# Flash-style cross attention on one core: value sums of eight heads in one PSUM bank, exponentials of 1536 columns, 4 of 40 units as a polynomial on VectorE, the four leftover keys in one tile

## The chip, the cores and the metric

The kernel runs on one core of a Trainium2 chip. The metric is the device time of one execution in microseconds (us). The engines are TensorE (PE, matrix products; its weight loads are listed apart as PEld), ScalarE (ACT, here the exponentials), VectorE (DVE), GpSimd (POOL, here copies of values) and SyncE (SP, which issues most DMAs). SBUF is the on-chip memory, PSUM the eight banks of 128 x 512 floats into which TensorE writes.

## What is computed

The reference is a decoder of four layers on 1024 query rows of width 128 and a context of 6404 rows. Three of the four layers (L0, L1, L3) have softmax attention with 16 heads of 8 channels over the whole context; L1 also attends causally to the queries themselves. Between the attention stages stand feed-forward layers that the change doesn't touch.

```python
# 16 heads of 8 channels, x: 1024 rows, ctx: 6404 rows, a mask over the keys
q = x_norm @ Wq + bq ; k = ctx @ Wk + bk ; v = ctx @ Wv + bv
scores = einsum("qhd,khd->hqk", q, k) * 8 ** -0.5      # L1: 1024 more keys, causal
out = softmax(scores, axis=-1) @ v                     # per head
x = x + tanh(gate) * (out @ Wo + bo)
```

## The kernel before

**Tiling.** The context is cut into 51 chunks of 128 keys (`NC`); the last holds only 4 keys (`LAST`). An attention stage is four sweeps (`SWEEPS`): eight of the sixteen heads (`hh`) by 512 of the 1024 queries (`qh`). A sweep goes over all 51 chunks; in L1 four or eight chunks of own keys (`nx`) follow, the later of them over fewer and fewer columns, with one more product with a triangular tile (`stair`) that masks them. Twelve sweeps make 612 chunks of context and 24 of own keys. A *unit* is one head by one chunk, 128 keys x 512 queries. A chunk has eight units.

**Scores.** A unit's score is one matmul (L1517) over 35 rows: even heads use the upper half of the array's rows (from 0), odd heads the lower half (from 64). Two units, an even and an odd one, make a pair; a pair fills two PSUM banks, and three such slots (banks 0 to 5) are used in turn. `scores(b, c, j)` waits for the exponential of three pairs ago.

**Exponentials.** ACT makes one exponential for each pair (L1334), 1024 columns, four for each chunk. No maximum is taken off the scores (a branch that would do it is not entered with these inputs), and the sum of the exponentials comes from a column of ones among the values.

**Values.** Four units make a value batch (L1530): four matmuls in float32 with 32 columns of weights each, one on each quarter of the array's columns, over the 512 queries. A float32 matmul stands as two records in the trace, so a batch is eight. Batches of heads 0 to 3 add up in bank 6, those of heads 4 to 7 in bank 7. At a sweep's end DVE copies both banks out (L1736). Before the next sweep's first value batch PE waits for that copy.

**Order.** PE's order is written out: two pairs of scores, one value batch, two pairs, one batch, in a loop of three chunks (`TC`). Keys for the next chunks are loaded by SP (L1059, L1062: three DMAs for each chunk) into three buffers `kr`; POOL copies values into `vr` (L1207). In front of a stage SP loads the first three chunks of keys, then sends `bound` through a DMA (L1079) to DVE, which makes a flag (L1698) that PE, ACT and SP read before they begin the sweeps. DVE has no work within a sweep. ACT issues the constant rows of `kr` and the weights (L1270 to L1287) in the preparation ahead of the first stage. After a stage PE transposes `accs`, four blocks for each 128 queries (L1567).

## Time and profile before

| | before |
|---|---|
| median of three runs | 3404.56 us (3403.14 to 3406.20) |
| the profiled execution | 3407.25 us |
| its span, first to last instruction | 3405.3 us |
| mean granted TensorE clock | 0.948 of full speed |
| busy: PE, ACT, DVE, POOL | 3077.4, 2607.3, 355.2, 202.7 us |
| first exponential of stage L0 to the last copy of its sums | 189.50 to 953.99 us |

A busy share of PE counts matmuls with modelled ends, so it does not say that the array streams all that time. The three attention stages make up about 2400 us of the span, and within them the pattern of a chunk repeats over and over; what a change of that pattern costs is read from one period of it.

### The profile page before, as it was taken

How to read it: one execution, taken by the hardware profiler on the slowest of the kernel's cores; microseconds unless marked ns; L12 is line 12 of the kernel's file. 1: busy time of each engine (PE TensorE's matmuls, PEld its weight loads, DVE VectorE, ACT ScalarE, POOL GpSimd, SP SyncE). 2: the span in 40 equal slices, each digit the busy share in tenths (PEclk: the TensorE clock that was granted, in tenths of full speed). 3: DMA queues.
4: the chain of work that ended last, by engine and by line, in shares of the span. 5: the costliest groups of instructions: out<-in, count | busy, mean ns of one | idle time of the engine just before them, and what ended most of it. 6: DMA issues, size and time to landing. Idle time of an engine off the chain costs nothing.

```text
span 3405.3 us, 62250 instructions
## 1 busy us (share of the span) xinstructions
PE 3077.4 (90%) x18851; PEld 1118.2 (33%) x18851; DVE 355.2 (10%) x951; ACT 2607.3 (77%) x3015; POOL 202.7 (6%) x726
## 2 busy tenths in 40 slices
PE   6689999999989799999999998969989999999988
PEld 3322222222233522222223224645622222222256
DVE  4410000000022500000000001342210000000021
ACT  3379999999933399699797994322289999999932
POOL 2000000000000000000000000010000000000000
PEclk9889999999979899799898997979999999999989
DMA  6701111111130011011010112101001111111100
GB/s 188 203 30 37 37 37 34 37 37 36 37 90 0 15 37 37 27 37 37 29 37 29 37 37 65 33 29 35 26 28 37 37 37 36 37 36 36 37 29 28
DMA packets 146162, 147.00 MB, mean 43 GB/s; under 512 B 15420, under 2 KB 98864, under 8 KB 146088
## 3 DMA queue, kind: packets, MB, share of 16 engines
q1 hardware_dynamic: 140304, 144.16, 13.8%
q10 hardware_dynamic: 5784, 1.88, 0.2%
q8 instruction: 43, 0.70, 0.1%
q14 instruction: 31, 0.25, 0.0%
HBM read 116.61 MB, written 29.37 MB: 43 GB/s over the span
## 4 chain that ended last, share of the span: by engine, by line
ACT 33%; issue 31%; PE 28%; ACTq 3%; DVE 3%; POOL 1%; DMA 0%; SPq 0%; DVEq 0%; POOLq 0%
ACT probs L1334 32%; PE PS L597 5%; PE PS L581 5%; PE PS L1530 3%; PE PS L1517 3%; PE PS L583 2%; PE PS L815 1%; ACTq L1329 1%; PE PS L803 1%; PE PS L1380 1%; ACTq L1338 1%; PE PS L1519 1%; PE PS L1390 1%; ACTq L1332 1%; PE PS L1444 1%
## 5 line engine op out<-in xcount | busy, mean ns | idle before, releaser
L1334 ACT ACTIVATE probs<-PS 128x1024 f32<-128x1024 f32 (+2 forms) x2544 | 2323.5, 1064 | 127.9 <-PE PS L1517 70.2
L1530 PE MATMUL PS<-probs,vr 128*32 128x512 f32 (+2 forms) x10176 | 1372.7, 612 | 135.5 <-ACT probs L1334 10.9
L1517 PE MATMUL PS<-qs,kr 35*128 35x512 f32 (+2 forms) x5088 | 985.2, 452 | 33.8 <-issue 15.7
L1517 PEld LDWEIGHTS PS<-qs,kr 35*128 35x128 f32 x5088 | 406.1, 189 | 1123.3 <-ACT probs L1334 1025.6
L1530 PEld LDWEIGHTS PS<-probs,vr 128*32 128x32 f32 x10176 | 203.0, 109 | 683.4 <-ACT probs L1334 645.6
L1207 POOL COPY vr<-vs 128x72 f32 (+1 forms) x636 | 159.7, 252 | 2881.8 <-PE PS L1530 2523.6
L1736 DVE COPY accs<-PS 128x1024 f32<-128x1024 f32 x12 | 14.7, 1225 | 2439.3 <-PE PS L1530 2439.3
L624 ACT ACTIVATE probs<-PS 128x512 f32<-128x512 f32 x96 | 57.3, 597 | 132.3 <-PE PS L581 71.8
L624 ACT ACTIVATE accs<-PS 128x512 f32<-128x512 f32 x96 | 57.3, 597 | 120.6 <-PE PS L581 63.2
L581 PE MATMUL PS<-xT,wide 128*128 128x512 f32 x256 | 125.6, 609 | 0.7 <-ACT xT L314 0.7
L597 PE MATMUL PS<-wide,accs 128*128 128x128 f32 x768 | 91.7, 281 | 5.0 <-DVE kf L656 5.0
L597 PEld LDWEIGHTS PS<-wide,accs 128*128 128x128 f32 x768 | 91.2, 198 | 11.5 <-issue 11.5
L597 PEld LDWEIGHTS PS<-wide,probs 128*128 128x128 f32 x768 | 88.3, 192 | 7.7 <-issue 7.7
L597 PE MATMUL PS<-wide,probs 128*128 128x128 f32 x768 | 88.3, 275 | 0.0
L768 ACT ACTIVATE probs<-PS,cols_w 128x512 f32<-128x512 f32 x48 | 32.8, 687 | 71.1 <-PE PS L804 71.1
L311 ACT ACTIVATE ln_sd<-ln_ve 128x8 f32<-128x8 f32 x8 | 1.7, 208 | 88.7 <-DVE ln_ve L285 88.7
L583 PE MATMUL PS<-xT,wide 128*128 128x512 f32 x128 | 66.7, 603 | 0.0
L581 PEld LDWEIGHTS PS<-xT,wide 128*128 128x128 f32 x256 | 46.7, 194 | 60.3 <-issue 33.8
L320 PE MATMUL PS<-ident,xn 128*128 128x128 f32 x64 | 17.0, 434 | 53.7 <-DVE xn L295 53.7
L656 DVE SCALAR_TENSOR_TENSOR kf<-PS,egate,kf 128x128 f32<-128x128 f32 x176 | 47.6, 344 | 153.8 <-PE PS L597 153.8
L581 PE MATMUL PS<-h_T,wide 128*128 128x512 f32 x128 | 59.9, 613 | 1.9 <-ACT h_T L933 1.9
L1244 ACT ACTIVATE kparts<-PS,bqk 128x384 fp32r<-128x384 f32 x27 | 16.0, 592 | 53.1 <-PE PS L1371 26.7
(269 smaller groups left out, 1206.5 us busy)
## 6 DMA issues: line engine op xcount, KB each, us to landing
kr<-key_pieces SPq DMA_DIRECT2D x1272, 64.0 KB
key_pieces<-kparts SPq DMA_DIRECT2D x36, 288.0 KB, 4.4
kr<-mask_strips SPq DMA_DIRECT2D x636, 4.0 KB
key_pieces<-probs SPq DMA_DIRECT2D x32, 288.0 KB, 4.7
vs<-values SPq DMA_DIRECT2D x2, 3672.0 KB, 15.5
values<-v_next SPq DMA_DIRECT2D x9, 432.0 KB, 5.3
wide<-in_L_ffn_w SPq DMA_DIRECT2D x28, 128.0 KB, 2.1
values<-probs SPq DMA_DIRECT2D x8, 432.0 KB, 5.3
```

What stands on the lines that cost most here:

```text
L581: last = te.matmul(PS[:, slot(m, k, i), :], eA[i][:, P * c:P * c + P], hT[:, 512 * half:512 * half + 512], start=True, stop=True)
L583: last = te.matmul(PS[:, 3 + slot(m, k, i), :], eB[i][:, P * c:P * c + P], hT[:, 512 * half:512 * half + 512], start=True, stop=True)
L597: last = te.matmul(PS[:, 6 + n // 4, n % 4 * P:n % 4 * P + P], moe_hid[i][:, S * c + P * n:S * c + P * n + P], eC[i][:, P * c:P * c + P], ...
L624: nc.scalar.activation(moe_hid[i][:, S * c + 512 * half:S * c + 512 * half + 512], PS[:, slot(m, k, i), :], m.func).then_inc(h_act, 1)
L656: last = v.scalar_tensor_tensor(moe_acc[:, P * n:P * n + P], o, g, moe_acc[:, P * n:P * n + P], ALU.mult, ALU.add)
L803: te.matmul(PS[:, u % 2, :], fw1[net][:, P * c:P * c + P], xT[:, cols], start=True, stop=True)
L815: last = te.matmul(o, fw2[net][:, D * c:D * c + D], hid[u % 4], start=(c == 0), stop=False)
L1207: g.tensor_copy(vr[b][:, :, 0:VC], vs[:, bass.ds(c, 1), h0:h0 + H // 2, :].rearrange("p o h v -> p (o h) v")).then_inc(v_copied, 1)
L1329: act.wait_ge(s_ready, 4 * c + (s.pairs + p + 1))
L1334: sc.activation(prob[p][:, :, q0:], PS[:, 2 * slot:2 * slot + 2, q0:], ACT.Exp, scale=SCALE).then_inc(p_ready, 1)
L1517: last = te.matmul(o, kr[b][own, j, :], qs[own, T8 // 2 * s.hh + j, 512 * s.qh + q0:512 * s.qh + 512], start=True, stop=not late)
L1530: last = te.matmul(PS[32 * j:32 * j + 32, 6 + g, q0:], vr[b][:, 4 * g + j, :], prob[2 * g + j // 2][:, j % 2, q0:], start=(first and c == ...
```

## The change

It rewrites the sweeps. Names: a *round* (`ITER`, 10 for each sweep) is five chunks, 40 units.

- The 4 keys of the last chunk leave the chunk pattern. All eight heads' leftover keys stand in one tile, `k_left`: four accumulating score matmuls (`left_scores`), one exponential of 512 columns (`exps_left`), one matmul of 128 columns of weights (`left_values`) for each sweep.
- ACT takes 36 units of a round in 12 groups of three (`GROUP`), each one exponential of 1536 columns; two slots of three banks (0 to 2, 3 to 5) are used in turn, so `scores(i, gr)` waits for the exponential of two groups ago. Four value buffers `prob` (`RING`) replace four of two units.
- The other four units (heads 0 to 3 of the third chunk) go to DVE: `score_d` writes one unit to bank 6, DVE reads it (L2077, L2079), and for two units at a time does five operations of 1024 columns (shift, three steps of a polynomial, the last product into `prob_d`, which lies in `accs`). `values_d` sums them with scaled values `vd`.
- All value batches add up in bank 7: the weights of a head are shifted by 16 of its 32 columns for heads 4 to 7.
- Base two: the query weights are scaled by `QSCALE`, ACT's scale is ln 2.
- Keys have five buffers; the third chunk's are loaded in three pieces. The leftover keys and values are loaded by 12 and 16 small DMAs in front of each stage, ahead of the DMA of `bound`. `wo` is turned through DRAM, with DMAs on ACT's queue.

```diff
+KB = 5
+ITER = (NC - 1) // KB
+GROUP = 3
+BY_ACT = ((0, 0), (0, 1), (1, 0), (1, 1), (2, 1), (3, 0), (3, 1), (4, 0), (4, 1))
+RING = 4
...
+                sp.wait_ge(v_final, a + 1)
+                load_left_values()
                 sp.wait_ge(bound_ready, a + 1)
                 sp.dma_start(bound_row[0:1, :], bound[32 * a:32 * a + H, 0:1]).then_inc(bound_in, 16)
...
-                            sc.activation(prob[p][:, :, q0:], PS[:, 2 * slot:2 * slot + 2, q0:], ACT.Exp, scale=SCALE).then_inc(p_ready, 1)
+                        sc.activation(prob[gr % RING], PS[:, bank:bank + GROUP, :], ACT.Exp, scale=LN2).then_inc(p_ready, 1)
...
+                    def scores(i, gr, first=False):
+
+                        if not (first and s.w == 0 and gr < 2):
+                            pe.wait_ge(p_ready, i * GPI + (s.groups + gr - 1))
...
+                    def score_d(i, j):
...
+                        if n or not isinstance(i, int):
+                            pe.wait_ge(d_read, i * DPI + n)
+                        score(PS[:, 6, :], 2, j).then_inc(d_ready, 1)
...
-                    with pe.Fori(1, NTILE) as i:
...
+                    with pe.Fori(1, ITER) as i:
+                        scores(i, 0)
+                        score_d(i, 0)
+                        values(s, i - 1, 7)
+                        scores(i, 1)
+                        values(s, i - 1, 8)
+                        scores(i, 2)
+                        scores(i, 3)
+                        score_d(i, 1)
+                        values(s, i, 0)
...
+                        scores(i, 5)
+                        score_d(i, 2)
+                        values(s, i, 2)
+                        scores(i, 6)
+                        values_d(s, i - 1)
...
+                        scores(i, 10)
+                        score_d(i, 3)
+                        scores(i, 11)
+                        values(s, i, 6)
...
+                    def two_units(i, p, first=False):
...
+                        if not (first and s.w == 0 and p == 0):
+                            dve.wait_ge(d_done, m - 1)
+                        for k in range(2):
+                            cols = slice(512 * k, 512 * k + 512)
+                            dve.wait_ge(d_ready, i * DPI + (n + k + 1))
+                            v.tensor_scalar(d_bits[:, cols], PS[:, 6, :], LOWEST, ROUND_AT, ALU.max, ALU.add).then_inc(d_round, 1)
+                            dve.wait_ge(d_round, i * DPI + (n + k + 1))
+                            v.scalar_tensor_tensor(d_x[:, cols], d_bits[:, cols], ROUND_AT, PS[:, 6, :], ALU.subtract, ALU.subtract).then_inc(d_read, 1)
+                        v.tensor_scalar(d_r.bitcast(I32), d_bits.bitcast(I32), 23, None, ALU.logical_shift_left).then_inc(d_shift, 1)
+                        dve.wait_ge(d_read, i * DPI + (n + 2))
+                        v.scalar_tensor_tensor(d_q, d_x, QA, d_x, ALU.add, ALU.mult).then_inc(d_q1, 1)
+                        dve.wait_ge(d_shift, m)
+                        v.scalar_tensor_tensor(d_bits, d_x, QC, d_x, ALU.add, ALU.mult).then_inc(d_q2, 1)
+                        dve.wait_ge(d_q1, m)
+                        v.scalar_tensor_tensor(d_q, d_q, QB, d_r, ALU.add, ALU.mult).then_inc(d_r1, 1)
+                        dve.wait_ge(d_q2, m)
+                        dve.wait_ge(d_r1, m)
+                        if s.w or not first:
+                            dve.wait_ge(d_used, i + ITER * s.w)
+                        v.scalar_tensor_tensor(prob_d[:, 2 * p:2 * p + 2, :].rearrange("p j n -> p (j n)"), d_bits, QD, d_q, ALU.add, ALU.mult).then_inc(d_done, 1)
```

PE, the loop of a sweep, before: half a chunk is two pairs (L1517) and a value batch (L1530).

```order
L1511 ISA
L1517 MATMUL PS<-qs,kr0 128x512 x2
L1511 REGISTER_ALU
L1517 MATMUL PS<-qs,kr0 128x512 x2
L1526 ISA
L1530 MATMUL PS<-probs,vr2 32x512 x4
```

PE, the same place in the changed kernel, from group 3 (`x3`, keys of chunk 1) over the second unit for DVE (the single matmul on `kr2`) to the batch after group 5. L1774 is a score, L1737 a value batch.

```order
L1774 MATMUL PS<-qs,kr1 128x512 x3
L1795 REGISTER_ALU
L1774 MATMUL PS<-qs,kr2 128x512
L1730 ISA
L1737 MATMUL PS<-probs,vr0 32x512 x4
L1780 REGISTER_ALU
L1774 MATMUL PS<-qs,kr1 128x512 x3
L1737 MATMUL PS<-probs,vr0 32x512 x4
```

A batch now follows one group of three units, not two pairs, and the single score stands in PE's queue ahead of batch 0, with its wait for DVE's second read of the unit before it (`d_read`).

DVE, the sweeps of the first stage, before, between the branch on the flag and the division that follows the stage: the four copies of the sums (L1736).

```order
L1729 CAST mparts<-mneg 128x128
L1731 TENSOR_TENSOR mparts<-mneg,mparts 128x128
L1701 UNCONDITIONAL_BRANCH
L1736 COPY accs<-PS 128x2x512 x4
L1740 RECIPROCAL rden<-PS 128x16
L1741 TENSOR_TENSOR xn<-PS,rden 128x128
```

DVE, one pair of units in the changed loop, with the semaphores that each row waits for. `kf`, `h_T`, `xT`, `xn` serve as scratch; `accs` is `prob_d`.

```order
L2077 TENSOR_SCALAR kf<-PS 128x512 [waits d_ready]
L2079 SCALAR_TENSOR_TENSOR h_T<-kf,PS 128x512 [waits d_round]
L2080 TENSOR_SCALAR xn<-kf 128x1024
L2082 SCALAR_TENSOR_TENSOR xT<-h_T 128x1024 [waits d_read]
L2084 SCALAR_TENSOR_TENSOR kf<-h_T 128x1024 [waits d_shift]
L2086 SCALAR_TENSOR_TENSOR xT<-xT,xn 128x1024 [waits d_q1]
L2091 SCALAR_TENSOR_TENSOR accs<-kf,xT 128x1024 [waits d_used,d_r1,d_q2]
```

What moved: between the reads of one pair of units and the reads of the next, DVE has five long operations in its queue, and PE's next `score_d` but one waits behind them. (The first two rows stand twice in the program, once for each unit.)

SP, in front of a stage, before: nine DMAs of keys, then `bound`.

```order
L1059 DMA kr2<-key_pieces 32x1x512 x2
L1062 DMA kr2<-mask_strips 2x512
L1079 DMA bound_row<-bound 1x16x1
L1081 TENSOR_LOAD flag
L1081 ISA x2
L1082 COMPARE_AND_BRANCH
```

SP, the same place in the changed kernel, from the last of four such groups of leftover keys on.

```order
L1158 DMA k_left<-key_pieces 16x4x4 x2
L1160 DMA k_left<-mask_strips 1x4x4
L1168 DMA v_left<-vs 4x9 x16
L1197 DMA bound_row<-bound 1x16x1
L1199 TENSOR_LOAD flag
L1199 ISA x2
L1200 COMPARE_AND_BRANCH
```

The DMA of `bound` now stands behind 40 more: 12 for keys, 12 for the leftover keys, 16 for the leftover values.

## Rows read from the trace of the kernel before

**Rows 1.** The page, busy time by engine (share of the span), instructions.

```profile
PE 3077.4 (90%) x18851; PEld 1118.2 (33%) x18851; DVE 355.2 (10%) x951; ACT 2607.3 (77%) x3015; POOL 202.7 (6%) x726
```

**Rows 2.** Timeline of ACT, first sweep: start, length, what, idle before.

```profile
205.60 175.19 ACT L1334 ACTIVATE probs<-PS 128x1024 f32<-128x1024 f32 x191 [0.33 <-PE PS L1517]
```

**Rows 3.** Timeline of PE, 700 to 702 us, full clock.

```profile
699.96 1.06 PE L1530 MATMUL PS<-probs,vr 128*32 128x512 f32 x8
700.96 0.73 PE L1517 MATMUL PS<-qs,kr 35*128 35x512 f32 x4
```

**Rows 4.** Timeline of PE, own keys of L1, full clock.

```profile
1616.66 0.50 PE L1517 MATMUL PS<-qs,kr 35*128 35x512 f32 x1
1617.09 0.23 PE L1519 MATMUL PS<-stair,ident_b 128*128 128x128 bf16 x1
```

**Rows 5.** Timeline of PE and of ACT, 577 to 583 us, half clock.

```profile
577.07 1.93 PE L1530 MATMUL PS<-probs,vr 128*32 128x512 f32 x8
578.93 1.22 PE L1517 MATMUL PS<-qs,kr 35*128 35x512 f32 x4
580.08 1.93 PE L1530 MATMUL PS<-probs,vr 128*32 128x512 f32 x8
...
582.78 1.94 ACT L1334 ACTIVATE probs<-PS 128x1024 f32<-128x1024 f32 x2 [1.07 <-PE PS L1517]
```

**Rows 6.** Groups by line and shape: count, busy us, mean ns (exponentials, operations of DVE).

```profile
L1334 ACT ACTIVATE probs<-PS 128x768 f32<-128x768 f32 x16 | 13.0, 811 | 11.1 <-PE PS L1519 11.1
L1334 ACT ACTIVATE probs<-PS 128x256 f32<-128x256 f32 x16 | 6.2, 384 | 21.0 <-PE PS L1519 21.0
L642 DVE TENSOR_TENSOR probs<-probs,PS 128x512 f32<-128x512 f32 x32 | 22.0, 688 | 61.5 <-ACT probs L624 61.5
L654 DVE TENSOR_SCALAR kf<-PS,egate 128x128 f32<-128x128 f32 x16 | 4.3, 343 | 29.9 <-PE PS L597 29.9
L1645 DVE TENSOR_SCALAR vs<-vs,valid_last 128x144 f32<-128x144 f32 x2 | 0.6, 284 | 0.0
```

**Rows 7.** Timeline of DVE between stages: dependent long operations, and eight independent short ones.

```profile
2119.48 1.23 DVE L873 TENSOR_TENSOR accs<-xn 128x1024 f32<-128x1024 f32 x1
2120.74 1.22 DVE L874 TENSOR_REDUCE ln_ve<-accs 128x8 f32<-128x1024 f32 x1
2151.84 2.16 DVE L656 SCALAR_TENSOR_TENSOR kf<-PS,egate,kf 128x128 f32<-128x128 f32 x8 [4.99 <-PE PS L597]
```

**Rows 8.** Timeline of PE over the end of the second sweep.

```profile
570.49 1.06 PE L1530 MATMUL PS<-probs,vr 128*32 128x512 f32 x8 [0.77 <-ACT probs L1334]
```

**Rows 9.** Windows: us, busy of PE, PEld, DVE, ACT, POOL, granted clock, DMA share, GB/s.

```profile
573.00:587.00 14.00, 13.74 (x58) 3.31 (x58) 0.00 (x0) 9.80 (x12) 0.50 (x2) 0.51 0.07 20
760.00:772.00 12.00, 9.66 (x72) 2.57 (x68) 1.23 (x1) 10.41 (x12) 0.76 (x3) 1.00 0.09 29
2867.00:2870.30 3.30, 3.30 (x16) 0.70 (x12) 0.00 (x0) 2.83 (x3) 0.00 (x0) 0.52 0.13 41
```

**Rows 10.** Timeline: first exponential and last copy of sums, stages L0 and L3.

```profile
189.50 1.02 ACT L1334 ACTIVATE probs<-PS 128x1024 f32<-128x1024 f32 x1 [10.52 <-PE PS L1517]
953.99 1.23 DVE L1736 COPY accs<-PS 128x1024 f32<-128x1024 f32 x1 [187.50 <-PE PS L1530]
2484.95 1.94 ACT L1334 ACTIVATE probs<-PS 128x1024 f32<-128x1024 f32 x2 [4.66 <-PE PS L1517]
3244.99 1.22 DVE L1736 COPY accs<-PS 128x1024 f32<-128x1024 f32 x1 [190.04 <-PE PS L1530]
```

**Rows 11.** Timeline around the flag of L0: SP's and ACT's DMA issues, DVE.

```profile
131.42 0.58 ACT L1244 ACTIVATE kparts<-PS,bqk 128x384 fp32r<-128x384 f32 x1 [10.49 <-issue]
173.30 0.59 SPq L1079 DMA_DIRECT2D bound_row<-bound  x1
183.67 0.29 DVE L1695 TENSOR_TENSOR kv_sum<-PS,kv_mask 128x128 f32<-128x128 f32 x1 [2.04 <-PE PS L1467]
183.88 0.15 DVE L1697 TENSOR_REDUCE bound_max<-bound_row 1x1 f32<-1x16 f32 x1
```

More of the change, by code:

```diff
@@ L1121, in _ @@
+                    with sp.Fori(1, ITER) as i:
+                        next_keys(i)
+                    for xc in range(s.nx):
+                        b = xc % KB
+                        sp.wait_ge(s_ready, s.groups + (GPI * (ITER - 1) + KEYS_FREE[b] if xc < KB else GPI * ITER + 4 * (xc - KB) + 4))
+                        if b == 2:
+                            sp.wait_ge(d_ready, DPI * ITER * (s.w + 1))
+                        load_keys(b, NC + xc, s.hh, kr_in[b])
                 end = SWEEPS[4 * a + 3]
-                sp.wait_ge(s_ready, end.pairs + 4 * end.n)
+                sp.wait_ge(s_ready, end.groups + end.n_groups)
@@ new lines, in _ @@
+                    if prev:
+                        pool.wait_ge(d_used, ITER * s.w)
+                    copy_scaled(2)
+                    with pool.Fori(1, ITER) as i:
+                        for b in range(KB):
+                            pool.wait_ge(pv_done, i * BPI + (s.batches - BPI + VALUES_FREE[b]))
+                            copy_values(b, i * KB + b, 4 if b == 2 else 0)
+                        pool.wait_ge(d_used, i + ITER * s.w)
+                        copy_scaled(i * KB + 2)
@@ L1220, in _ @@
+                    for xc in range(s.nx):
+                        b = xc % KB
+                        pool.wait_ge(pv_done, s.batches + (BPI * (ITER - 1) + VALUES_FREE[b] if xc < KB else BPI * ITER + 2 * (xc - KB) + 2))
+                        copy_values(b, NC + xc)
                 between_pool(pool, a)
@@ L1562, in _ @@
[L1562 removed]
+                    scores(0, 0, True)
+                    if prev:
+                        if not prev.nx:
+                            values(prev, ITER - 1, BPI - 2)
+                        left_scores(prev)
+                    scores(0, 1, True)
+                    if prev:
+                        last_values(prev)
+                    scores(0, 2, True)
+                    if prev:
+                        left_values(prev)
+                        pe.wait_ge(left_done, s.w)
@@ new lines, in _ @@
+                    score_d(0, 0)
+                    scores(0, 3, True)
+                    if prev:
+                        values_d(prev, ITER - 1)
+                    scores(0, 4, True)
+                    score_d(0, 1)
+                    values(s, 0, 0, True)
+                    values(s, 0, 1)
+                    scores(0, 5, True)
+                    values(s, 0, 2)
+                    scores(0, 6, True)
+                    score_d(0, 2)
+                    scores(0, 7, True)
@@ new lines, in _ @@
+                    for gr in range(4 * s.nx):
+                        scores_own(gr // 4, gr % 4)
+                        if gr < 2:
+                            values(s, ITER - 1, BPI - 2 + gr)
+                        elif gr % 2:
+                            quad = gr // 2 - 1
+                            values_own(s, quad // 2, quad % 2)
+                    if s.w % NSW == NSW - 1:
+                        if not s.nx:
+                            values(s, ITER - 1, BPI - 2)
+                        left_scores(s)
+                        last_values(s)
+                        left_values(s)
+                        values_d(s, ITER - 1)
```

459 lines of the change are left out of this document (326 added, 133 removed).

## The prediction

> **What bounds the kernel now.** First the busy shares: PE 90%, ACT 77%, DVE 10% [rows 1]. The full clock helps to sort the first two. In a sweep ACT never rests: 191 exponentials in 175.19 us, one every 0.917 us, 3.67 us for a chunk [rows 2]. PE's part of half a chunk is a value batch and two pairs. From a batch's start to the scores behind it go 1.00 us [rows 3]. Of the scores a single one on one half of the array takes 0.43 us until something else can start [rows 4]; the second slot of the two adds 512 columns at 2.4 GHz, 0.21 us. So PE needs 1.64 us of the 1.83 that two exponentials take, and ACT is the bound, by little. The half clock is the test: there PE goes from batch to batch in 3.01 us, and ACT idles 1.07 us of it [rows 5]. Two halves of the array work at once: four scores of 512 columns would alone take 1.71 us at 1.2 GHz, and the whole step from scores to batch is 1.15 us [rows 5].
>
> **The size of the part that is replaced.** Stage L0 runs from 189.50 to 953.99 us, 764.5 us, of which 204 chunks x 3.67 are 748.5 and 16.0 are the turns between sweeps and the half clock behind one of them; L3 gives 760.0, so 11.5 [rows 10]. For three stages I take out 3 x 748.5 = 2245.5, and 42 for the turns. The own keys of L1 stay about as they are.
>
> **A round of 40 units, engine by engine.** Before, five chunks cost 18.35 us.
>
> *ACT.* Between 256 and 768 columns an exponential grows by 811 - 384 = 427 ns for 512 columns [rows 6], 0.834 ns each; 1536 columns repeat every 0.917 + 0.427 = 1.34 us, twelve of them 16.1 us.
>
> *PE.* Scores alternate between the array's halves, so three units take two slots, as four did: every group costs as much as two pairs. Ten batches with a group each are 10 x 1.64 = 16.4; the two groups and the single scores that share a run with another add 1.5. Together 17.9 us. PE is now slower than ACT, and still below 18.35.
>
> *DVE.* An operation of 512 columns takes 0.69 us [rows 6], one of 1024 takes 1.22, and the next one that depends on it starts 0.03 after its end (2119.48 + 1.23 against 2120.74) [rows 7]. Independent ones start earlier: eight of 0.34 us take 2.16 us in all, so 0.26 apart, 0.08 less than their length [rows 7]. All DVE rows of 512 and 1024 columns run at one column in 1.04 ns. The shift has no scalar tensor and one source in SBUF; the nearest row, 144 columns in SBUF, takes 284 ns where 128 columns from PSUM take 343 [rows 6], which fits half the time for each column. I take 0.69 for its 1024 columns, with 1.22 as the upper bound. For two units: reads 0.72 + 0.60 + 0.72 + 0.60, shift 0.60, then 1.14 + 1.14 + 1.26 + 1.26 = 8.0 us, 16.1 us a round. The Trainium skill ("VectorE: DVE Perf Modes", "Mode 2x_2P") states that a float32 operation with one source runs two elements a cycle in SBUF and not from PSUM; no row here has that shape at full size. By that rule the shift costs 0.69; without it 1.22, which would be 64 us more over the kernel.
>
> So each engine alone has less to do than 18.35 us. The loop through both decides. DVE reads unit 0 of the next round only after the last product of this round's second pair, and PE's `score_d` of unit 1 stands in its queue behind group 3 and waits for that read (`d_read`). PE can't pass it, and the batches and groups behind it wait too.
>
> - From PE's issue of unit 3 to that of the next unit 1: score until ready 0.5; reads 0.72 + 0.60; shift 0.60; 1.14 + 1.14; 1.26 + 1.26; reads of unit 0: 0.72 + 0.69 + 0.04. Sum 8.7 us. PE's own work in that stretch (batches 6, 7, 8, groups 11, 0, 1, 2, 3) is 6.3 us, so it pauses for 2.4 us.
> - From unit 1 to unit 3 PE has seven batches and seven groups in front of it: 7 x 1.64 = 11.5 us. DVE needs 0.5 + 6.7 us for its first pair there and waits for `values_d` besides, reads unit 2, then rests until unit 3 comes.
>
> A round is 8.7 + 11.5 = **20.1 us**, 1.8 more than before. With the shift at 1.22 it is 20.7; with every fixed part of DVE's operations at nothing, 11.5 + 0.5 + 6.9 = 18.9.
>
> **The clock.** The pause is one block of 2.4 us in each round. At a turn before, PE's gap ahead of the last batch is 0.77 us [rows 8], and behind three of nine turns the clock fell to 1.2 GHz, for 3.3 us at the shortest and 14 at the longest, while others stayed at 2.4 [rows 9]. Bounds: no drop, and 14 us of half clock in every round. The pause is longer than any gap at a turn, so I take one drop for each round, and the shortest length, since a full batch and group run follows: 3.3 x (1 - 1.64 / 3.01) = 1.5 us, less the rest DVE gains meanwhile: 1.4. A round is then 21.5 us, 120 of them 2580 us. The Trainium skill ("TensorE: Matmul & The Clock Gate", "HAM oscillation") describes a kernel whose every block starts at the half clock because the wait ahead of it throttles TensorE. By it the drop would come in every round (21.5 us); by the six turns that kept the clock it would not (20.1). The trace has both outcomes.
>
> **The rest.** Per sweep: the leftover tile has four scores in one run (about 1.1 us of PE), a full batch (1.0) and an exponential of 512 columns (0.6) in place of the 51st chunk; at the turn DVE copies 512 columns before it reads unit 0, and `score_d` waits for that. I take 4 us a sweep, between 2 and 7: 48. In front of L0, 40 more DMAs at 0.59 stand ahead of `bound`: 23.6 us, less the 4 us by which it was early (DVE came from L1695 to the flag in 0.2 us, long after the DMA) [rows 11]: 19. In front of L1 the 16 DMAs of leftover values follow the key stores, 9.4 us, some 3 of them free: 6. ACT's queue in the preparation gets 14 more DMAs, and its work there already waits 10.49 us for issue [rows 11]: 10. The transposes behind a stage are halved: -7. Sum: +28.
>
> **Forecast.** 3407.25 - 2245.5 - 42 + 2580 + 48 + 28 = 3775.75; the profiled execution stands 2.7 above the median, so **3773 us**, 10.8% slower.
>
> **Rivals.**
>
> 1. *The loop without the clock.* The pause costs only itself, as at most turns before [rows 9]. 120 x 1.4 = 168 less: 3605. For it: six of nine turns kept the clock, and the array streams densely in the rest of a round.
> 2. *Longer drops.* Half clock for 7 us in each round adds 3.2 - 1.4 = 1.8: 3989. At 14 us it is 4.9 more: 4360. Against it: half-clocked PE takes so long that DVE is no longer late, so there is no second pause. For it: the 14 us at 573 [rows 9].
> 3. *DVE is quick enough (the other side).* If the stretch from unit 3 to the next unit 1 takes DVE under 6.3 us, PE never pauses, and the round is PE's 17.9: 3.6 less than forecast, 432 in all: 3341, faster by 1.9%. It decides at 2.4 us out of 8.7. Against it: that stretch has 4 x 512 + 5 x 1024 columns, 7.5 us at 1.04 ns even without the fixed parts, 6.9 if the shift runs at double rate. It needs a DVE rate that no row shows, or PE steps that overlap more than rows 3 and 4 do; then the bound moves on to ACT's 16.1 and the time to 3125.
> 4. *ACT alone sets the time.* Someone who reads only that ACT never rests [rows 2] expects 12 x 1.34 x 120 = 1930 in place of 2245, so about 3125. PE's 1.64 for each batch and group speaks against it: it would have to be under 1.4.
>
> **Chances.** Forecast 43% (3680 to 3880 with the turns and the shift at their bounds), rival 1 25% (3560 to 3680), rival 2 12%, rival 3 with PE as the bound 13%, ACT as the bound 7%. The range from 3340 to 3980 holds the first two, half of the third and most of rival 3 with PE, 0.8 together; the forecast's own is 3680 to 3880. About 0.2% is what a measurement of this kernel can tell from no change. Faster by more than that 0.17, within it 0.02 (rival 3 with a small pause left), slower 0.81.
>
> **What the profile of the changed kernel would show.** ACT: 1080 long exponentials less than 1.5 us each, with idle time ahead of them ended by PE. PE: one pause in each round, ahead of the single score of unit 1, put down to DVE's second operation (L2079); batch to group 1.00 us. DVE: busy about 16 us of a round, its rest ahead of L2077, put down to PE. Granted clock in the sweeps well below 1.00, dips of some us at the round's pace; without them rival 1 holds. If the pause is missing, the length of L2082 to L2091 was wrong. If batches and groups stand closer than 1.64 us, PE's term was. If ACT has no idle time, rival 4 was right. The first exponential of L0 should stand near 219 us.
>
> **What would make it wrong.** The largest term is the length of a round: 0.1 us of it is 12 us of the time. The drops are counted from three events and could be off by their whole price either way.

## The result, and the profile after

| | before | after |
|---|---|---|
| median | 3403.86 us (3403.14 to 3406.20) | 4294.16 us (4232.53 to 4332.76) |
| profiled execution, its span | 3407.25, 3405.3 us | 4296.56, 4294.4 us |
| mean granted TensorE clock | 0.948 | 0.764 |
| busy PE, ACT, DVE | 3077.4, 2607.3, 355.2 us | 3942.4, 2419.1, 2272.5 us |

The ratio is 1.252, 95% interval 1.237 to 1.267: the change makes the kernel a quarter slower, 521 us more than was predicted, and outside the range. The ratio is taken over the two executions within 1.5% of the fastest (4232.53 and 4291.75 us). Differences from this kernel below are taken from the median of all four, which spread over 100 us. The 889 us between the two spans lie like this: 24.8 ahead of the first exponential (214.33 against 189.50), 270 in stage L0, 292 in L1, 301 in L3, 1 in all the rest. It is the sweeps.

The page of after, busy time and groups, answers to [rows 1, 6]:

```profile
PE 3942.4 (92%) x18587; PEld 1381.6 (32%) x18587; DVE 2272.5 (53%) x3113; ACT 2419.1 (56%) x2019; POOL 345.3 (8%) x839
...
L1518 ACT ACTIVATE probs<-PS 128x1536 f32<-128x1536 f32 x1440 | 2052.8, 1451 | 1114.4 <-PE PS L1774 1061.3
L1774 PE MATMUL PS<-qs,kr 35*128 35x512 f32 (+1 forms) x4992 | 1469.0, 565 | 183.1 <-DVE h_T L2079 142.4
...
L2080 DVE TENSOR_SCALAR xn<-kf 128x1024 int32<-128x1024 int32 x240 | 164.6, 686 | 0.0
```

ACT idles 1114 us ahead of its exponentials, nearly all for PE. PE idles only 183 us ahead of scores, 142 of it for DVE's second read: 81 pauses, of 1.8 us on average. A pause itself is thus a sixth of the loss. The rest shows in PE's timeline (L1774 is a score, L1737 a value batch; start, length):

```profile
234.69 0.73 PE L1774 MATMUL PS<-qs,kr 35*128 35x512 f32 x3
235.35 1.07 PE L1737 MATMUL PS<-probs,vr 128*32 128x512 f32 x8
236.34 1.42 PE L1774 MATMUL PS<-qs,kr 35*128 35x512 f32 x6
239.65 0.49 PE L1774 MATMUL PS<-qs,kr 35*128 35x512 f32 x1 [1.88 <-DVE h_T L2079]
240.07 1.93 PE L1737 MATMUL PS<-probs,vr 128*32 128x512 f32 x8
241.93 1.22 PE L1774 MATMUL PS<-qs,kr 35*128 35x512 f32 x3
243.08 1.93 PE L1737 MATMUL PS<-probs,vr 128*32 128x512 f32 x8
244.94 1.22 PE L1774 MATMUL PS<-qs,kr 35*128 35x512 f32 x4
246.09 1.45 PE L1737 MATMUL PS<-probs,vr 128*32 128x512 f32 x8
247.47 0.73 PE L1774 MATMUL PS<-qs,kr 35*128 35x512 f32 x3
```

Ahead of the pause a batch takes 1.07 us and leads to scores after 1.00, as in [rows 3]. Unit 1 (`x1`) waits 1.88 us. Right behind it the batch takes 1.93 us, the half-clock length of [rows 5], until the one at 246.09, in which the clock comes back. The windows of after (columns as in [rows 9], PEclk is the last but two):

```profile
240.10:246.90 6.80, 6.80 (x28) 1.57 (x31) 5.39 (x6) 2.07 (x2) 0.00 (x0) 0.50 0.06 20
311.80:349.30 37.50, 37.50 (x143) 10.03 (x143) 20.75 (x24) 19.14 (x14) 2.63 (x6) 0.50 0.06 21
1004.70:1107.10 102.40, 102.40 (x385) 27.30 (x383) 52.96 (x60) 53.59 (x38) 7.51 (x18) 0.50 0.07 21
469.30:721.50 252.20, 238.02 (x1208) 66.07 (x1209) 160.98 (x182) 171.60 (x122) 24.81 (x60) 0.78 0.08 27
```

A drop mostly lasts 6.8 us, and now and then 37.5 us, more than a round, in which PE does not rest at all. Four drops in the sweeps last longer still, three 102.4 us and one 136.5, and hold two or three whole rounds, of 32.3 us each. I take the length of a round from the start of its third exponential to that of the next round's, 108 rounds in twelve sweeps: 41 have 6.8 us of half clock and take 23.7 us; 36 hold the greater part of a long drop, 30.7 us of half clock, and take 33.4; the other 31, most of which hold the end of a long drop, have 3 to 12 us and take 21.7. The mean is 26.34 us, with 14.8 us of half clock.

DVE over the same pause, and the setup of L0, which answer to [rows 7, 11]:

```profile
231.24 0.69 DVE L2077 TENSOR_SCALAR kf<-PS 128x512 f32<-128x512 f32 x1 [3.10 <-PE PS L1774]
...
232.57 0.68 DVE L2080 TENSOR_SCALAR xn<-kf 128x1024 int32<-128x1024 int32 x1
...
236.81 1.23 DVE L2091 SCALAR_TENSOR_TENSOR accs<-kf,xT 128x1024 f32<-128x1024 f32 x1
238.18 0.69 DVE L2077 TENSOR_SCALAR kf<-PS 128x512 f32<-128x512 f32 x1
238.90 0.69 DVE L2079 SCALAR_TENSOR_TENSOR h_T<-kf,PS 128x512 f32<-128x512 f32 x1
...
206.05 0.56 SPq L1197 DMA_DIRECT2D bound_row<-bound  x1
...
214.33 2.79 ACT L1518 ACTIVATE probs<-PS 128x1536 f32<-128x1536 f32 x2 [26.41 <-PE PS L1774]
```

From the first read of unit 3 (231.24) DVE goes without rest through its chain to the read of the next unit 0 (end 239.59), and 0.06 us later PE issues unit 1. The chain takes 8.35 us, where the terms of the prediction add up to 8.13.

### The profile page after: what moved, and what is told of

Its sections match the earlier page's. It is cut to its first block and busy times, and to the rows that moved or that the text cites. A ratio compares the mean times of both kernels' runs of the same rounds, so it can differ in the third digit from the quotient of the medians.

```text
span 4294.4 us, 62487 instructions
## 1 busy us (share of the span) xinstructions
PE 3942.4 (92%) x18587; PEld 1381.6 (32%) x18587; DVE 2272.5 (53%) x3113; ACT 2419.1 (56%) x2019; POOL 345.3 (8%) x839
## 5 line engine op out<-in xcount | busy, mean ns | idle before, releaser
L1518 ACT ACTIVATE probs<-PS 128x1536 f32<-128x1536 f32 x1440 | 2052.8, 1451 | 1114.4 <-PE PS L1774 1061.3
L1774 PE MATMUL PS<-qs,kr 35*128 35x512 f32 (+1 forms) x4992 | 1469.0, 565 | 183.1 <-DVE h_T L2079 142.4
L1737 PE MATMUL PS<-probs,vr 128*32 128x512 f32 x8640 | 1588.1, 819 | 0.0
L1774 PEld LDWEIGHTS PS<-qs,kr 35*128 35x128 f32 x4992 | 642.1, 237 | 1804.3 <-ACT probs L1518 823.5
L2077 DVE TENSOR_SCALAR kf<-PS 128x512 f32<-128x512 f32 x480 | 331.9, 691 | 727.5 <-PE PS L1774 699.2
L2091 DVE SCALAR_TENSOR_TENSOR accs<-kf,xT 128x1024 f32<-128x1024 f32 x240 | 294.2, 1226 | 455.0 <-PE PS L1746 442.9
L1737 PEld LDWEIGHTS PS<-probs,vr 128*32 128x32 f32 x8640 | 193.3, 122 | 528.3 <-issue 355.2
L2079 DVE SCALAR_TENSOR_TENSOR h_T<-kf,PS 128x512 f32<-128x512 f32 x480 | 329.8, 687 | 16.3
L2082 DVE SCALAR_TENSOR_TENSOR xT<-h_T 128x1024 f32<-128x1024 f32 x240 | 296.1, 1234 | 0.0
L2084 DVE SCALAR_TENSOR_TENSOR kf<-h_T 128x1024 f32<-128x1024 f32 x240 | 293.5, 1223 | 0.0
L2086 DVE SCALAR_TENSOR_TENSOR xT<-xT,xn 128x1024 f32<-128x1024 f32 x240 | 291.9, 1216 | 0.0
```

What stands on the lines that cost most here:

```text
L1518: sc.activation(prob[gr % RING], PS[:, bank:bank + GROUP, :], ACT.Exp, scale=LN2).then_inc(p_ready, 1)
L1737: last = te.matmul(PS[32 * j:32 * j + 32, 7, :], vr[b][:, 32 * (4 * q + j) + lo:32 * (4 * q + j) + lo + 32], prob[n // GROUP % RING][:, n ...
L1774: return te.matmul(o, kr[b][own, h // 2, :], qs[own, T8 // 2 * s.hh + h // 2, 512 * s.qh + q0:512 * s.qh + 512], start=True, stop=not more)
L2077: v.tensor_scalar(d_bits[:, cols], PS[:, 6, :], LOWEST, ROUND_AT, ALU.max, ALU.add).then_inc(d_round, 1)
L2079: v.scalar_tensor_tensor(d_x[:, cols], d_bits[:, cols], ROUND_AT, PS[:, 6, :], ALU.subtract, ALU.subtract).then_inc(d_read, 1)
L2082: v.scalar_tensor_tensor(d_q, d_x, QA, d_x, ALU.add, ALU.mult).then_inc(d_q1, 1)
```

## The experiments

The theory after the result: DVE's chain makes PE pause once in a round, and this pause, not the work, brings PE down to 1.2 GHz for much longer than it lasts. Rivals: the dense new pattern (groups of three with single scores) drops the clock by itself; or ACT, DVE or the keys' loads set the time. The ratios are against the kernel before, timed beside each batch of runs (3400.9 to 3402.3 us).

### A shorter chain

e1_short_chain leaves two of the five long operations out, so the values of DVE's units are not the exponential's.

```diff
                         dve.wait_ge(d_shift, m)
-                        v.scalar_tensor_tensor(d_bits, d_x, QC, d_x, ALU.add, ALU.mult).then_inc(d_q2, 1)
                         dve.wait_ge(d_q1, m)
-                        v.scalar_tensor_tensor(d_q, d_q, QB, d_r, ALU.add, ALU.mult).then_inc(d_r1, 1)
-                        dve.wait_ge(d_q2, m)
-                        dve.wait_ge(d_r1, m)
```

> Two of the five long DVE operations of each pair of units are left out (the second factor of the polynomial and the product with the power of two), so the exponentials of 4 of 40 units are wrong; all else is done. It takes 1.14 + 1.26 = 2.4 us off the stretch from unit 3 to the next unit 1. Theory (the loop through DVE and PE makes a pause, and the pause makes the clock fall): no pause of over 0.3 us ahead of unit 1, rounds of 17.9 us at full clock, total 3340 to 3420 us. Rival (the clock falls for a reason of its own, such as groups of three units that leave half of the array idle in every second slot): drops stay, rounds of 22 to 25 us, total above 3900.

Measured: 3487.27 us, ratio 1.024 (1.021 to 1.027). 2.3 us less of DVE's work in each half round takes 807 us off the kernel. 89 of 108 rounds have no half clock and take 18.48 us. The time is 67 us over the theory's 3420: a round is 0.6 us longer than the 17.9 expected, and 19 rounds still have half clock, seven of them 26 us or more. It is far from the rival's 3900. PE, ACT and the loads do what they did, so none of them alone holds the changed kernel at 4294.

### The pause filled

e2_filled_pause leaves everything as it is and puts two matmuls over zero weights where PE would pause.

```diff
                         scores(i, 3)
+                        for _ in range(2):
+                            te.matmul(PS[:, 7, :], zero_one[:, 0, :], qs[:, 0, 0:512].bitcast(F32), start=False, ...)
                         score_d(i, 1)
```

> Two matmuls with weights of zero, which add nothing to the sums, stand ahead of the score of unit 1 in each round of the loop, about 1.9 us of TensorE work in the pause. Theory (the clock falls because of the pause): the pause stays as long but is filled, rounds of 20.2 to 20.5 us, granted clock in the sweeps near 1.00, total 3600 to 3700 us. Rival (the clock falls for another reason): drops stay, total as the changed kernel or longer, above 4200.

Measured: 3688.4 us, ratio 1.086 (1.083 to 1.089). PE's timeline of it:

```profile
309.10 1.42 PE L1774 MATMUL PS<-qs,kr 35*128 35x512 f32 x6
310.46 1.98 PE L1856 MATMUL PS<-qs,zero_one 128*128 128x512 f32 x4
312.37 0.50 PE L1774 MATMUL PS<-qs,kr 35*128 35x512 f32 x1
312.80 1.06 PE L1737 MATMUL PS<-probs,vr 128*32 128x512 f32 x8
```

Unit 1 is as late as ever (1.91 us behind the group), but PE does not rest, and the batch behind takes 1.06 us and not 1.93. 96 of 108 rounds are without half clock and take 20.61 us. Useless work makes the kernel 606 us faster. The time is inside the theory's range, the round 0.1 us over its own (20.2 to 20.5). That is the cleanest proof: the loop through DVE costs 20.6 - 18.4 = 2.2 us a round, the pause's effect on the clock another 5.7.

### The pause taken away by the order

e3_even_units moves the four single scores to behind groups 0, 2, 6 and 8 (they stood behind 0, 3, 5, 10) and `values_d` from 6 to 4.

```diff
                         scores(i, 2)
+                        score_d(i, 1)
                         scores(i, 3)
-                        score_d(i, 1)
...
                         scores(i, 8)
+                        score_d(i, 3)
...
                         scores(i, 10)
-                        score_d(i, 3)
```

> Only the order in PE's loop is changed: the four units for DVE stand behind groups 0, 2, 6, 8 (before: 0, 3, 5, 10) and their value batch behind group 4 (before: 6), so that unit 3 comes 3.3 us earlier. Theory: DVE has done its chain before PE wants the read of unit 0, the pause goes, rounds are PE's 17.9 us, total 3340 to 3420 us. Rival (DVE is the bound whatever the order): rounds stay above 20 us, total above 3600.

Measured: 3508.11 us, ratio 1.033 (1.029 to 1.037), 88 us over the theory's 3420. 86 rounds without half clock take 18.38 us, 77 of them 18.31 to 18.34 and seven 18.22, against 17.9 expected. The same work in another order is 786 us faster. What is left comes partly from first rounds, whose order this edit doesn't touch; the timeline of PE there:

```profile
420.23 0.49 PE L1774 MATMUL PS<-qs,kr 35*128 35x512 f32 x1 [1.47 <-DVE h_T L2079]
...
438.94 1.36 PE L1774 MATMUL PS<-qs,kr 35*128 35x512 f32 x4 [2.56 <-DVE h_T L2079]
440.23 1.93 PE L1737 MATMUL PS<-probs,vr 128*32 128x512 f32 x8
```

### The units on ACT

e4_units_on_act gives DVE nothing in the loop; ACT takes the four units as exponentials of 512 columns (single scores behind groups 3, 5, 7, 9).

```diff
+                        sc.activation(prob_d[:, j, :], PS[:, 6, :], ACT.Exp, scale=LN2).then_inc(d_read, 1)
```

> The polynomial is undone: ACT takes the four units as exponentials of 512 columns from bank 6, DVE has no work in the sweeps; single scores behind groups 3, 5, 7, 9, their batch behind group 2. Theory: ACT has 12 x 1.34 + 4 x 0.49 = 18.1 us a round and PE 17.9, rounds of 18.1 to 18.6 us, clock near 1.00, total 3370 to 3470 us, about that of the kernel before. Rival (the group structure itself is what costs): rounds above 20 us, total above 3600.

Measured: 3557.58 us, ratio 1.040 (1.034 to 1.045). Its window over the same stretch of L0:

```profile
471.00:720.00 249.00, 238.26 (x1543) 71.25 (x1536) 0.69 (x1) 237.34 (x207) 19.02 (x77) 1.00 0.11 35
```

The full clock all through (after has 0.77 in this stretch), ACT busy 237 and PE 238 of 249 us, a round 19.37 us. The time was missed by 88 us: a round is 0.8 us longer than expected, and L1 has 253 us of half clock. ACT and PE wait for each other in turn (in the round from 499.98 to 519.26 us ACT waits 0.62 us for PE, and PE 0.79 us for ACT), so neither is the bound alone; no run takes that apart. 19.37 is more than the 18.35 of before, and 1.0 us more than a round of e3: that is what four units on DVE are worth, if they cause no pause. The full clock with the groups of three in place speaks against the rival that the new pattern drops it.

### A part of the pause, and more of it

e5_one_filler is e2 with one filler. e6_longer_pause puts `score_d(i, 3)` behind group 11 in place of 10, nothing else.

> The changed kernel with one matmul over zero weights (0.43 us of PE) ahead of the single score of unit 1, so that PE's pause there is some 1.5 us where it was 1.9 with none and under 1.1 with two (which left 96 of 108 rounds without half clock). Theory (how long the clock stays down follows from the length of the pause): rounds between the two cases, most of them with a short drop of 3.4 us or none, 20.3 to 22.5 us, and a time of 3700 to 3950 us. Rival (any pause above a microsecond costs the same 6.8 us and now and then a whole round): 23.5 us and more for a round, 4200 us or more, as the changed kernel.

> The changed kernel with the single score of unit 3 one group later (behind group 11 in place of 10), nothing else: PE has one batch and group less to do between unit 3 and the next unit 1, and pauses some 1.6 us longer, 3.5 us at full clock. By the loop alone the round is 8.7 + 13.1 = 21.8 us. Theory (a longer pause keeps the clock down longer): at the 6.8 us of half clock per round of before it would be 24.9 us a round and 4450 us in all; with more rounds wholly at half clock up to 31.5 us a round and 4900 us. Rival (the pause's length makes no difference to the drops, and at half clock PE is late enough to hide it): 4300 us, as the changed kernel.

Measured: e5 3741.55 us, ratio 1.098 (1.095 to 1.102); e6 4482.12 us, ratio 1.322 (1.314 to 1.329). PE in e5, and then in e6:

```profile
307.96 1.12 PE L1855 MATMUL PS<-qs,zero_one 128*128 128x512 f32 x2
309.83 0.49 PE L1774 MATMUL PS<-qs,kr 35*128 35x512 f32 x1 [0.74 <-DVE h_T L2080]
310.25 1.06 PE L1737 MATMUL PS<-probs,vr 128*32 128x512 f32 x8
```

```profile
345.40 0.59 PE L1774 MATMUL PS<-qs,kr 35*128 35x512 f32 x1 [2.37 <-DVE h_T L2079]
```

The filler took 1.1 us (not the 0.43 that I had given it), and with 0.74 us of pause left 81 of 108 rounds have no half clock, 20.56 us each. The time is in the theory's range, but the pause of 1.5 us that the two theories differ on was not run. Of 103 pauses of 0.74 to 0.8 us, 11 were followed by half clock. In e6 the pause is 2.37 us (3.5 expected). The short drops are still 6.8 us, so a longer pause doesn't lengthen them; but the long ones, 37.5 us in after, are 41.0, and in its first sweeps they come with every second drop instead of every third. The time lies at the low end of the theory's range (4450 to 4900), though not by its mechanism, a longer short drop. The mean round goes up from 26.34 to 27.50 us: one with 6.8 us of half clock takes 24.4 us (23.7 in after), and 40 hold the greater part of a long drop where 36 did. The kernel takes 188 us more.

### The pause alone, in the kernel before

e10_pause_in_before is the kernel before; once in its loop of three chunks PE waits for two operations of DVE on scratch. e11_short_pause_in_before has only the first of them.

```diff
                             values((b - 1) % TC, i * TC + (b - 1), 1)
+                            if b == 0:
+                                pe.wait_ge(pause_end, i + (NTILE - 1) * s.w)
                             scores(b, c, 2, ld)
...
+                    with dve.Fori(1, NTILE) as i:
+                        dve.wait_ge(pv_done, i * (2 * TC) + s.groups)
+                        v.scalar_tensor_tensor(kf[:, 0:512], idle_src[:, 0:512], 1.0, idle_src[:, 0:512], ...)
+                        v.scalar_tensor_tensor(h_T[:, :], idle_src, 1.0, idle_src, ...).then_inc(pause_end, 1)
```

> The kernel before, with a pause of PE alone: once in each turn of its loop (three chunks, 11.0 us) PE waits behind a value batch until DVE has made two operations of 512 and 1024 columns on scratch, some 1.9 us, as long as the pause in the changed kernel. Nothing else is changed. PE has 9.84 us of work in 11.0, so the pause alone makes the turn 11.75 us, 192 turns 3550 us. Theory (a PE pause of this length drops the clock, whatever the kernel): 6.8 us of half clock behind each costs 3.1 more, 14.8 us a turn and 4130 us; with stretches wholly at half clock up to 4800. Rival (the drops belong to the changed pattern, groups of three with single scores): 3450 to 3600 us, clock near 0.93.

> As e10_pause_in_before with the 512-column operation alone, a pause of some 0.75 us. PE's 9.84 + 0.75 us fit in the 11.0 that ACT needs. Theory (pauses under a microsecond leave the clock alone, as the 0.74 us in e5_one_filler): 3400 to 3440 us. Rival (any regular pause drops it): 3600 us or more.

Measured: e10 4536.49 us, ratio 1.332 (1.329 to 1.336), clock 0.740; e11 3582.92 us, ratio 1.052 (1.048 to 1.056), clock 0.950. PE in e10 (L1519 scores, L1532 batch):

```profile
303.72 1.06 PE L1532 MATMUL PS<-probs,vr 128*32 128x512 f32 x8
306.78 0.73 PE L1519 MATMUL PS<-qs,kr 35*128 35x512 f32 x4 [1.99 <-DVE h_T L1742]
307.44 1.06 PE L1532 MATMUL PS<-probs,vr 128*32 128x512 f32 x8
308.44 0.91 PE L1519 MATMUL PS<-qs,kr 35*128 35x512 f32 x4
309.32 1.93 PE L1532 MATMUL PS<-probs,vr 128*32 128x512 f32 x8
```

Nothing of the change is in this kernel, and its time is inside the theory's 4130 to 4800: half clock for 6.8 or 10.2 us behind a pause, and 33 times for 37.5 us. So the drops do not belong to the new pattern. Not every pause brought one: 159 of the 192 pauses (1.99 to 2.08 us) began at the full clock, and the clock fell within 3.6 us of 121 of them; in after it fell at all 80. In e11 PE pauses 0.81 to 0.89 us once in 11.75, the clock fell at none of 191, and its mean is as before, 0.950 against 0.948. But its time was missed (3440 at most was expected), the 0.75 us are not hidden. PE and ACT in e11:

```profile
301.79 0.73 PE L1519 MATMUL PS<-qs,kr 35*128 35x512 f32 x4 [0.82 <-DVE kf L1741]
```

```profile
302.32 11.11 ACT L1336 ACTIVATE probs<-PS 128x1024 f32<-128x1024 f32 x12 [0.64 <-PE PS L1519]
```

A turn takes 11.75 us, the 11.0 of before and the 0.75 us of DVE's operation. My reading, which no run tests: PE has 0.19 us to spare in each step, but it can't save them up, since it waits for free banks, and a single stop of several steps' slack reaches ACT.

### What else the change costs: setup and turns

e7_left_loads_later is e3 with the 28 small DMAs of leftover keys and values sent in rounds 1 to 3 of a stage's first sweep. e8_even_turns adds a more even first round; its loop has the single scores behind 1, 3, 7, 9. e9_best_order takes the loop of e3 again and puts unit 1 of a first round ahead of group 4. e12_filled_turns adds a filler of 256 columns ahead of the two single scores of a sweep for which PE still waits. The lines shown are from e9.

```diff
-                with sp.Fori(1, ITER) as i:
+                for i in range(1, late):
+                    next_keys(i)
+                    if i == 1:
...
+                        load_left(hh)
...
+                        load_left_values(range(8 * i - 16, 8 * i - 8))
+                with sp.Fori(late, ITER) as i:
...
                     scores(0, 2, True)
                     if prev:
+                        values_d(prev, ITER - 1)
                         left_values(prev)
                         pe.wait_ge(left_done, s.w)
                     score_d(0, 0)
                     scores(0, 3, True)
-                    if prev:
-                        values_d(prev, ITER - 1)
+                    values(s, 0, 0, True)
+                    score_d(0, 1)
                     scores(0, 4, True)
-                    score_d(0, 1)
...
```

> e3_even_units with SP's 28 small DMAs for the leftover keys and values moved out of the way of the DMA of bound, into rounds 1 to 3 of each stage's first sweep. Theory (those DMAs delay the flag and with it the first exponential by the 24 us seen, 213.8 against 189.5): first exponential at 190 to 197 us, the time 15 to 24 us below e3_even_units, 3484 to 3493 us. Rival (another queue, ACT's with the added wo DMAs, holds the flag back as well): first exponential after 205 us, less than 10 us gained.

> e7_left_loads_later, with the first round of a sweep in a more even order too: the last sum of DVE's units ahead of that of the leftover keys, unit 0 right behind them, units 1 to 3 behind groups 4, 7 and 9 (the loop: 1, 3, 7, 9), value batches 0 and 1 each one group earlier. In e3_even_units PE pauses twice in a first round, 1.47 and 2.56 us, both put down to DVE's second read, and the clock falls for 6.8 us behind the second. Theory (these pauses and the drops they cause are what the turns cost): 2.5 to 5.5 us less for each of twelve sweeps, 3425 to 3460 us. Rival (the drops at a turn come from something else): no change against e7_left_loads_later, 3480 us or more.

> e8_even_turns with two things altered in PE's order: in the loop the single scores again behind groups 0, 2, 6, 8 and values_d behind 4, as in e3_even_units (whose round at full clock is 18.22 us, where the loop of e8_even_turns pauses 0.35 us at one single score, waits 0.2 us for ACT at others and needs 19.05), and in the first round unit 1 ahead of group 4. Theory (what is left over the kernel before is the length of the round and the first rounds): nine rounds of a sweep get 0.8 us shorter each, less 1 us of pause behind a first round: 60 to 85 us less than e8_even_turns, 3385 to 3415 us, about the kernel before. Rival (behind first rounds the clock falls again, as in e3_even_units): 3430 to 3470 us.

> e9_best_order with one matmul over zero weights and 256 columns (some 0.6 us) ahead of the two single scores where PE still pauses in every sweep, 0.84 us ahead of unit 3 in the first round and 0.88 ahead of unit 1 in the second; nothing else runs or moves. Theory (these two pauses start most of the half clock that is left in the sweeps, 20.5 us and twice 6.8 in sweeps 2 to 4 of L0): the half clock of sweeps 2 to 4 of L0 and L3 goes to 7 us or less each stage, and the time falls by 15 to 40 us to 3400 to 3425 us. Rival (these drops come from the turns themselves, the 0.67 us ahead of the first batch among them): less than 8 us gained, 3433 us or more. Either way the kernel before is at best equalled, since rounds take 18.22 us against 18.35 and the setup 10 us more.

Measured: e7 3493.98 us, ratio 1.026 (1.022 to 1.029); e8 3475.48, 1.023 (1.020 to 1.025); e9 3441.17, 1.013 (1.010 to 1.016); e12 3427.86, 1.008 (1.005 to 1.010).

The timeline of e7 around the flag:

```profile
188.22 0.59 SPq L1190 DMA_DIRECT2D bound_row<-bound  x1
...
192.63 0.16 DVE L2027 TENSOR_REDUCE bound_max<-bound_row 1x1 f32<-1x16 f32 x1 [1.77 <-DMA bound_row<-bound]
...
198.87 1.45 ACT L1523 ACTIVATE probs<-PS 128x1536 f32<-128x1536 f32 x1 [12.99 <-PE PS L1779]
```

`bound` goes out at 188.22 in place of 206.05, and the first exponential comes 15.5 us earlier than in after, at 198.87, 9.4 behind the kernel before; the time falls by 14 us. Both just miss the theory's ranges (190 to 197, and 3484 to 3493), and the intervals of the two ratios, 1.029 to 1.037 and 1.022 to 1.029, touch. The flag now waits only 1.77 us for that DMA; the query product ahead of the stage begins 7 us later than before, in the preparation in which ACT has 14 more DMAs to issue (no run takes those away).

e8 came out 18 us lower where 30 to 66 were expected, and its interval overlaps e7's, so that gain isn't clear of noise. It has less half clock (356 us of its whole profiled execution, e7 548), but its loop is worse, by a choice of mine; 101 of its rounds are without half clock, but take 19.05 us. PE's timeline has both:

```profile
306.24 0.50 PE L1779 MATMUL PS<-qs,kr 35*128 35x512 f32 x1 [0.35 <-DVE h_T L2084]
...
414.53 0.49 PE L1779 MATMUL PS<-qs,kr 35*128 35x512 f32 x1 [1.07 <-DVE h_T L2084]
...
416.91 1.93 PE L1742 MATMUL PS<-probs,vr 128*32 128x512 f32 x8
```

e9 came to 3441, inside the rival's range (3430 to 3470) and over the theory's (3385 to 3415): in its first two rounds PE pauses twice, and the clock falls.

```profile
800.85 0.50 PE L1779 MATMUL PS<-qs,kr 35*128 35x512 f32 x1 [0.85 <-DVE h_T L2084]
...
809.77 0.96 PE L1779 MATMUL PS<-qs,kr 35*128 35x512 f32 x4 [0.88 <-DVE h_T L2084]
810.67 1.79 PE L1742 MATMUL PS<-probs,vr 128*32 128x512 f32 x8
```

With both filled (e12) the half clock of sweeps 2 to 4 is gone in L0 (34 us in e9) and in L3 (20 us). The windows of two whole sweeps of e12, and of one of the kernel before, both at full clock:

```profile
397.00:585.20 188.20, 186.42 (x1210) 58.73 (x1210) 160.95 (x182) 168.56 (x121) 32.01 (x60) 1.00 0.11 36
585.20:773.40 188.20, 186.81 (x1212) 58.86 (x1213) 160.97 (x182) 168.57 (x121) 31.86 (x60) 1.00 0.11 36
```

```profile
382.90:571.60 188.70, 176.19 (x1226) 46.55 (x1228) 1.21 (x1) 187.14 (x204) 12.85 (x51) 1.00 0.11 37
```

That is what the change is worth without its pauses: 188.2 against 188.7 us a sweep. ACT's load falls from 187 to 169 us, PE's rises from 176 to 187, and the bound passes from ACT to PE at the same height. The 13 us that e12 gained on e9 just miss the 15 of the theory. None of these versions beats the kernel before: what e12 has over it, 27 us, is the setup (9 us) and half clock in first sweeps (L0 24 us against 15, L3 45 against 6) and in L1 (131 against 101).

## Why the prediction failed

- **The bound before, and ACT's term**: right, but for the count: there are 1440 long exponentials (12 for each of 120 rounds), not 1080. ACT's 1536 columns repeat every 1.34 to 1.35 us (three from start to end 4.14 us in e3, the last of them 1.45).
- **PE's round**: 17.9 us predicted, 18.3 in the even order. Two groups behind each other take 1.36 us and not 1.28, and a run of a group and a single score 0.74 to 0.89 where a group alone takes 0.66. That is the 18.35 of before again; by the windows of e12 and before, a sweep at full clock gains 0.5 us, 6 us in all. Here rival 4 (3125) and rival 3 (3341) part from what can be reached: e3 and e12 have no pause in most rounds, and stay over 3400.
- **DVE's durations**: right. The shift takes 686 ns; 0.69 was taken, by the Trainium skill's page "VectorE: DVE Perf Modes", section "Mode 2x_2P". The trace agrees with that page: 1024 columns with one source in SBUF take as long as 512 from PSUM (691 ns), and two-source operations of 1024 take 1216 to 1234.
- **The loop**: right in place and mechanism, the pause stands ahead of unit 1 and is put down to L2079. From unit 3 to the next unit 1 are 8.9 to 9.0 us (8.7 predicted), the pause is 1.88 (2.4), and a round through the loop without half clock is 20.56 to 20.61 us (20.1), by e5 and e2.
- **The clock: here it failed.** "I take one drop for each round, and the shortest length, since a full batch and group run follows." A fall at each pause was right (80 of the 81 pauses began at the full clock, and it fell at all 80). Its length, put at 3.3 us, was not: 6.8 us in the commonest round, 30.7 us in every third, 14.8 us a round on average. The price of it was right: (23.7 - 20.6) / 6.8 = 0.46 us for each us of half clock, against 1 - 1.64 / 3.01 = 0.455. A round is 26.34 us and not 21.5, and 4.84 over 108 rounds are 523 us, all of the 521 by which the time was missed: 0.5 of the 4.84 is the round without half clock (20.6 against 20.1), the other 4.3 the clock (5.7 against 1.4). Rival 2 was this case, with 7 us (3989) and 14 us (4360) as its prices; measured are 4294. It had 12%, because the argument against it was taken for a bound: "half-clocked PE takes so long that DVE is no longer late, so there is no second pause". That is true in the trace (in 37.5 us PE has no idle time), but a PE without idle time did not get its clock back for 37.5 us. [rows 9] had an instance in view, 14 us of half clock with PE busy in 13.74 of them. The range ended at 3980, below the cheaper price of that rival. The turns were misread too. Behind three of nine the clock fell, but that "others stayed at 2.4", and with it rival 1's "six of nine turns kept the clock", holds for three only: the other three, those of L1 at 1400, 1641 and 1860 us, have half clock ahead of them and behind, and the longest drop there is 37.5 us and not 14 (columns as in [rows 9]):

```profile
1385.50:1423.00 37.50, 32.80 (x143) 11.75 (x146) 1.22 (x1) 16.22 (x21) 1.12 (x5) 0.50 0.06 20
```

- **The Trainium skill's rule** ("TensorE: Matmul & The Clock Gate", "HAM oscillation"), that a wait ahead of each block makes the block start at the half clock: the waits of that page's kernel are longer, some 3 to 5 us by its diagram. In after the trace agrees for pauses of 1.79 to 1.88 us as well, by the 1.93-us batch behind the one shown; in e10, with 1.99 to 2.08 us, it agrees for 121 of 159. Here it was used for the count of drops only.
- **The rest** (turns, leftover tile, own keys, setup): all that is not in those 108 rounds, first rounds of sweeps included, was predicted within 3 us in sum. That is partly luck: what stands outside the 108 rounds took 10 us less than counted in L0 and L3 together and 9 more in L1, and the first exponential came at 214.3 (219 predicted).

**What stays open.** Why a drop ends after 6.8 us in one round and lasts 37.5 in another. In after they come mostly in a regular sequence (two short, one long), in e6 in a shorter one, and in e10 with 10.2 as well. The traces sort the lengths by the moment at which the granted clock falls, not by the pause. In after it fell 52 times 0.45 to 0.99 us behind the start of the late score, and each of these drops lasted 3.4 or 6.8 us; 27 times 1.00 to 1.27 us behind it, and each lasted 34 us or more; once 0.1 us ahead of it, for 136.5 us. In e10 a fall 0.48 to 0.65 us behind the start goes with 6.8 us, one 0.40 to 0.59 us ahead of it, still in the pause, with 37.5 (33 times) or 75.1 (once); in e6, of the pauses of 2.37 us, falls 0.22 to 0.41 us behind go with 6.8, and those from 0.09 behind to 0.32 ahead with 27 us or more. From one short drop of after to the next the fall comes some 0.24 us later, which fits the regular sequence. No run here sets that moment, or the length, by itself, so this is an order in the data and not a shown cause. Nor was it tried how to get the first rounds of a stage, where PE starts at 1.2 GHz, to the full clock sooner.

## What to carry to other kernels

Price a wait on PE by what the clock does behind it, not by its own length: 1.9 us once in 20 cost 5.7 us more, and to fill it with work over zero weights gave back 606 us. Where a loop goes through a second engine, spread the steps at which PE needs it over the round, and add up both halves of the way: 8.9 us did not fit under the 6.3 us that PE had there (five groups from unit 3 to the next unit 1), and in most rounds did when it was six groups. Before moving work off the bounding engine, add up the next one: here PE stood at 17.9 us by the sum and 18.3 on the chip, against 18.35, so the best that the pattern could gain was 6 us of 3404.

## What the runs showed of the hardware

- Pauses of PE at 2.4 GHz and what the granted clock did: 0.35 us each round (e8) left it at 1.00 in most rounds, 0.74 to 0.8 (e5) 92 times of 103, 0.81 to 0.89 (e11) all 191 times; two of 0.85 and 0.88 within 9 us (e9) were followed by 6.8 us at 1.2 GHz. 1.79 to 1.88 (after, all 72 of them) and 2.37 (e6, all 62) were followed by 1.2 GHz for 6.8 us or for 27 us and more; of 159 of 1.99 to 2.08 (e10) 121 were, for 3.4 to 75 us.
- Within one kernel the length of the drop went with the moment of the fall: in after 6.8 us or less for all 52 falls 0.45 to 0.99 us behind the pause's end, 34 us or more for all 27 at 1.00 to 1.27 us.
- At 1.2 GHz a PE that is busy without a gap stayed there for 37.5 us (window 311.80 to 349.30), and for 102.4 (1004.70 to 1107.10).
- A matmul over zero weights in float32, 128 rows and 512 columns, takes 0.95 us (two in 1.91 us) and is enough to keep the clock: with two of them in the pause (e2) 96 of 108 rounds had no half clock. 256 columns take 0.7.
- An integer shift of 1024 columns in SBUF takes 686 ns, an exponential of 1536 columns from PSUM 1451 ns and repeats every 1.34.
- SP issues a 4 x 9 DMA every 0.62 us (16 in 9.97 us).
